# Attention block over 16 images: the next input is exchanged behind the outputs, its statistics move into the scores, and one reciprocal moves ahead of the outputs

## What is computed

```python
h    = group_norm(x, 32 groups) * gn_w + gn_b
q, k, v = split(qkv_w @ h + qkv_b)            # each 512 x 1024
attn = softmax((q.T @ k) / sqrt(512), axis=-1)
o    = out_w @ (v @ attn.T) + out_b
out  = x + o
```

## Time and profile before

| | |
|---|---|
| median of 3 runs | 1997.63 us (1994.39 to 1999.02) |
| profiled execution | 1995.93 us |
| its span, first to last instruction | 1994.1 us |
| TensorE matmul busy | 1977.3 us (99%) |
| TensorE weight load busy | 1679.2 us (84%) |
| VectorE, ScalarE, GpSimd busy | 1644.5 us (82%), 1121.0 us (56%), 448.8 us (23%) |
| granted TensorE clock | 1.000 |
| DMA, mean over the span | 79 GB/s |

### The profile page before, as it was taken

How to read it: one execution, slowest core, us unless ns; L and a number is a source line. 1 busy time by engine, 2 the same in 40 slices (tenths; PEclk the granted TensorE clock), 3 DMA queues, 4 the chain that set the end, 5 groups by cost and what they waited for, 6 DMA issues and landing times. The chain is left out here.

```text
span 1994.1 us, 26069 instructions
## 1 busy us (share of the span) xinstructions
PE 1977.3 (99%) x9895; PEld 1679.2 (84%) x9895; DVE 1644.5 (82%) x2010; ACT 1121.0 (56%) x1431; POOL 448.8 (23%) x306
## 2 busy tenths in 40 slices
PE   9999999999999999999999999999999999999999
PEld 7888888888888888888888888887888888878788
DVE  8896987969879698796978879697796987969866
ACT  6564645646465564645656467464565646556461
POOL 1122040231412213131230401314022131221311
PEclk9999999999999999999999999999999999999999
DMA  6305143060431504324042330614306043150411
GB/s 176 128 7 138 49 75 118 6 159 28 75 118 22 170 2 75 118 54 139 6 86 101 70 123 6 146 41 75 118 11 165 17 75 118 20 172 2 75 33 54
DMA packets 102637, 157.89 MB, mean 79 GB/s; under 512 B 49377, under 2 KB 51265, under 8 KB 102513
## 3 DMA queue, kind: packets, MB, share of 16 engines
q0 software_dynamic: 31264, 73.15, 17.5%
q1 hardware_dynamic: 71248, 83.08, 12.9%
HBM read 85.57 MB, written 68.26 MB: 77 GB/s over the span
## 5 line engine op out<-in xcount | busy, mean ns | idle before, releaser
L459 PE MATMUL ring<-r_hi 128*128 128x512 f32 (+1 forms) x1724 | 657.3, 381 | 0.6 <-ACT ring L932 0.4
L460 PE MATMUL ring<-r_lo,r_hi 128*128 128x512 f32 (+1 forms) x1724 | 656.4, 381 | 0.0
L461 PE MATMUL ring<-r_hi,r_lo 128*128 128x512 f32 (+1 forms) x1724 | 656.3, 381 | 0.0
L459 PEld LDWEIGHTS ring<-r_hi 128*128 128x128 f32 x1724 | 324.2, 188 | 64.1 <-DVE r_lo L1478 2.1
L461 PEld LDWEIGHTS ring<-r_hi,r_lo 128*128 128x128 f32 x1724 | 324.2, 188 | 62.0
L460 PEld LDWEIGHTS ring<-r_lo,r_hi 128*128 128x128 f32 x1724 | 324.3, 188 | 61.1
L881 ACT ACTIVATE stage<-ring,keybias 128x512 f32<-128x512 f32 x256 | 175.2, 685 | 164.2 <-PE ring L461 161.5
L1171 POOL PARTITION_ALL_REDUCE stage<-stage x32 | 127.2, 3976 | 460.3 <-DVE stage L1531 460.3
L854 ACT ACTIVATE stage<-ring,by_tile 128x512 f32<-128x512 f32 x120 | 82.5, 687 | 245.9 <-PE ring L461 245.9
L1463 DVE TENSOR_TENSOR r_lo<-stage,r_hi 128x1024 fp32r<-128x1024 f32 x128 | 182.1, 1452 | 0.0
L459 PE MATMUL ring<-h_hi,r_hi 128*128 128x512 f32 x444 | 172.8, 389 | 0.1
(11 more groups left out here) (199 smaller groups left out, 3903.0 us busy)
## 6 DMA issues: line engine op xcount, KB each, us to landing
xs<-x_in SPq DMA_DIRECT2D x64, 512.0 KB, 6.2
out<-xs SPq DMA_DIRECT2D x60, 512.0 KB, 5.4
out<-run_max POOLq DMA_DIRECT2D x60, 256.0 KB, 5.7
inv<-inv_row SPq DMA_DIRECT2D x32, 256.0 KB, 4.1
out<-spare POOLq DMA_DIRECT2D x30, 256.0 KB, 6.9
out<-all_max POOLq DMA_DIRECT2D x30, 256.0 KB, 5.1
r_hi<-g_dram POOLq DMA_DIRECT2D x15, 512.0 KB, 6.4
r_lo<-g_dram POOLq DMA_DIRECT2D x15, 512.0 KB, 6.5
```

Source lines behind the costliest of these rows:

```text
L459: nc.tensor.matmul(ps_out, st_hi, m_hi, start=first, stop=False, skip_group_check=goes_on)
L460: nc.tensor.matmul(ps_out, st_hi, m_lo, start=False, stop=False, skip_group_check=goes_on)
L461: return nc.tensor.matmul(ps_out, st_lo, m_hi, start=False, stop=last, skip_group_check=goes_on)
```

## The change

- `change_input` (store `xs`, wait, load the next image) is a function now. Image 0's exchange stays in its scores; that of every later image `b + 1` (up to image 14) comes behind `spread_inverses(b, 1)` and ahead of `key_bias(b + 1)` in SyncE's list, that is at the start of T.
- `shift_input` of image `b + 1` comes behind ScalarE's four `h_combined_part`, ahead of its T work.
- From image 1 on, the eight `stats_part` go between VectorE's first maxima in S; `group_variance` comes behind them; `group_std_part` goes between ScalarE's copies of S2 and S3; `group_root` and `group_spread` ahead of four maxima, `affine_pair` ahead of the subtractions.
- `inverse(b, 1)` comes ahead of the scaled outputs of half 0.
- GpSimd's `load_u` waits for the end of product S2 of the scores with all its four loads; two of them went after A12 before.

```diff
@@ -413,20 +413,24 @@
                 for at, name in ((0, "a11"), (1, "a12")):
                     sp.dma_start(by_rows(u_dram[side, :, at, :]), u_raw(t, name).bitcast(FP32)).then_inc(s_u_out, DMA)
 
+            def change_input(b):
+
+                for k in range(CT):
+                    sp.wait_ge(s_shifted, b * CT + k + 1)
+                    sp.dma_start(out_v[b, :, k, :], xs[:, k, :]).then_inc(s_sent[k], DMA)
+                for k in range(CT):
+                    sp.wait_ge(s_sent[k], (b + 1) * DMA)
+                    sp.dma_start(xs[:, k, :], x_v[b + 1, :, k, :]).then_inc(s_x[k], DMA)
+
             def store_u_s2():
                 for n, (side, t) in enumerate(((0, r_hi), (1, r_lo))):
                     sp.wait_ge((s_uhi, s_ulo)[n], 2)
                     sp.dma_start(u_dram[side, :, 2, :], t[:, u_home(1, S2), :].bitcast(FP32)).then_inc(s_us2_out, DMA)
 
             for b in range(B):
-                for k in range(CT):
-                    if b + 1 < B:
-                        sp.wait_ge(s_shifted, b * CT + k + 1)
-                        sp.dma_start(out_v[b, :, k, :], xs[:, k, :]).then_inc(s_sent[k], DMA)
+                if b == 0:
+                    change_input(0)
                 if b + 1 < B:
-                    for k in range(CT):
-                        sp.wait_ge(s_sent[k], (b + 1) * DMA)
-                        sp.dma_start(xs[:, k, :], x_v[b + 1, :, k, :]).then_inc(s_x[k], DMA)
                     group_stats(b + 1)
                 if b == 1:
                     store_u_s2()
@@ -434,6 +438,8 @@
                 spread_inverses(b, 0)
                 own_sums(b, 1)
                 spread_inverses(b, 1)
+                if b + 2 < B:
+                    change_input(b + 1)
                 if b + 1 < B:
                     key_bias(b + 1)
 
@@ -1009,11 +1015,14 @@
                     if k == 0:
                         act.wait_ge(s_bias_out, (b + 1) * DMA)
                     copy_scores(b, P_A12, k, k, k, s_c11, CT)
-                    shift_input(b, k)
+                    if b == 0:
+                        shift_input(b, k)
 
                 act.wait_ge(s_tlo, splits(b + 1))
                 for i in range(CT):
                     copy_scores(b, P_S2, i, i, 8 + i, s_p2)
+                if 0 < b < B - 1:
+                    group_std_part(b + 1)
                 if b == 0:
                     for n, (a, count) in enumerate(((S1, 5), (S2, 6), (S3, 7), (S4, 8))):
                         g_sum_part(a, n, count)
@@ -1024,9 +1033,8 @@
                     copy_scores(b, P_S3, i, CT + i, 12 + i, s_p3)
                 for i in range(CT):
                     copy_scores(b, P_A22, i, CT + i, CT + i, s_c21)
-                if b + 1 < B:
+                if b == 0:
                     group_std_part(b + 1)
-                if b == 0:
                     exponential(b, 0, 0)
                     p_part(b, 0, 0)
                     exponential(b, 0, 1)
@@ -1091,6 +1099,8 @@
 
                             act.wait_ge(s_unit, unit(b, "A") + CT)
                         h_combined_part(b + 1, c)
+                    for k in range(CT):
+                        shift_input(b + 1, k)
 
         @block.gpsimd
         def _(pool):
@@ -1139,7 +1149,7 @@
                     nc.gpsimd.dma_start(t[:, at:at + 2, :], g_dram[side, :, :, :]).then_inc(s_gload, DMA)
 
             def load_u(b):
-                pool.wait_ge(s_unit, unit(b, "S") + 4 * P_A12 + 4)
+                pool.wait_ge(s_unit, unit(b, "S") + 4 * P_S2 + 4)
                 count = 1 if b == 1 else 2
                 if b == 1:
                     pool.wait_ge(s_u_out, 4 * DMA)
@@ -1148,7 +1158,6 @@
                 at = u_home(b, A12)
                 for side, t in ((0, r_hi), (1, r_lo)):
                     nc.gpsimd.dma_start(t[:, at:at + count, :], u_dram[side, :, 1:1 + count, :]).then_inc(s_uload, DMA)
-                pool.wait_ge(s_unit, unit(b, "S") + 4 * P_S2 + 4)
                 for side, t in ((0, r_hi), (1, r_lo)):
                     nc.gpsimd.dma_start(t[:, u_home(b, A11), :], u_dram[side, :, 0, :]).then_inc(s_uload, DMA)
 
@@ -1660,14 +1669,22 @@
                     key_bias(b)
                     t_sum_rest(b, S2)
                     for i in range(1, CT):
+                        if more:
+                            stats_part(b + 1, 2 * i - 2)
+                            stats_part(b + 1, 2 * i - 1)
                         max_step(b, 0, i, i, s_c11, b * 4 + i + 1)
                     t_sum_rest(b, S3)
+                    if more:
+                        stats_part(b + 1, 6)
+                        stats_part(b + 1, 7)
                     t_sum_rest(b, S4)
                 if b == 1:
                     u_sums()
-                if more:
+                if b == 0:
                     for q in range(CT * NB):
                         stats_part(b + 1, q)
+                elif more:
+                    group_variance(b + 1)
                 if b == 0:
                     for n, a in enumerate((S1, S2, S3, S4)):
                         g_sum_rest(a, n)
@@ -1678,28 +1695,31 @@
                     add_scores(b, P_S1, i, 12 + i, s_p3, s_c22)
                     if i > 0:
                         max_step(b, 1, i, CT + i, s_c22, b * 4 + i + 1)
+                if b > 0 and more:
+                    group_root(b + 1)
+                    group_spread(b + 1)
                 for i in range(CT):
                     max_step(b, 0, CT + i, CT + i, s_c21, b * 4 + i + 1)
-                if more:
+                if b == 0:
                     group_variance(b + 1)
                 for i in range(CT):
                     add_scores(b, P_S4, i, 8 + i, s_p2, s_c12)
                     max_step(b, 1, CT + i, i, s_c12, b * 4 + i + 1)
+                if b > 0 and more:
+                    affine_pair(b + 1)
 
                 for q in range(CT):
                     subtract_max(b, 0, q)
-                if more:
+                if b == 0:
                     group_root(b + 1)
                     group_spread(b + 1)
-                if b == 0:
                     for q in range(CT):
                         p_rest(b, 0, q)
                         first_v_rest(q)
                     first_v_rest(4)
                     subtract_max(b, 1, 0)
                     subtract_max(b, 1, 1)
-                    if more:
-                        affine_pair(b + 1)
+                    affine_pair(b + 1)
                     first_v_rest(5)
                     sum_tree(b, 0)
                     first_v_rest(6)
@@ -1739,11 +1757,11 @@
                     for k in range(CT):
                         h_rest(b + 1, k)
                     h_combined(b + 1)
+                inverse(b, 1)
                 for c in range(CT):
                     scale_output(b, 0, c)
                     if not more:
                         whole_output(0, c)
-                inverse(b, 1)
                 if more:
                     for k in range(CT):
                         key_dot(b + 1, k)
```

## The result

The changed kernel took 2004.06 us (median of 10 runs, 2000.04 to 2005.6) against 1997.97 us for the kernel before on the same chip (10 runs, 1993.66 to 2003.14): ratio 1.0028, interval 1.0016 to 1.0040. It is slower, where a gain of 9 us was forecast. The profiled execution took 2000.42 us with a span of 1998.6 us, 4.5 us more than before.

A forecast was written before the change was run, and what follows sets the result against it. TensorE was taken as the bound, with only its waits to win. Gains of 8.3 + 2.0 + 0.5 us less 1.4 and 0.4 us gave 9.0 us: 1988.6 us, own range 1985 to 1993, whole range 1984 to 2010 us.

The forecast's parts named there:

- the 0.9 us net delay of the fourth add: In T, half 0's fourth add lands 0.9 us later because it shares the DMA engines with stores of x.
- stores meet the last two adds: In T, shifts end near 1250, so stores of x overlap only half 0's last two adds; fourth lands 1.2 to 1.4 us late.
- the term of 1.4 us: At T's third product, 0.1 us of added TensorE wait in each of 14 images, a cost of 1.4 us.
- The reciprocal, 8.3 us: Between images, inv comes up to 2.4 us earlier, removing 9 TensorE waits at T's second product and their restarts: 8.3 us.
- What is late next: At T's third product, the lo part behind the last scaled output, held by the all_max add, has 0.8 us of slack.
- The statistics, 2.0 + 0.5 us: Statistics in S no longer wait for x: 2.0 us of waits in V and 0.5 us at T's third product gained.
- The floor of 12 us: Only TensorE's waits, 10.7 us, and some 1.5 us of restarts can be won: about 12 us, 0.6%.
- Rival 2: In T, adds wait behind stores, delayed 2 us or more, so the third product waits: 2004 to 2018 us, chance 0.2.
- The row on `U`: Loads of U beside stores of x landed in 7.3 us, G's without x in 6.5: 0.8 us for 512 KB.
- The rule quoted for it: An add's 2 KB row stands behind more than one 4 KB row of x, so the delay is over 1.4 us.
- Rival 4: Half 1's sum, not the reciprocal's place, sets its time, so the 7.4 us of waits stay: 1995 us, chance 0.03.

The follow-up runs named there:

- e2: The changed kernel with the input exchange of T behind the key bias in SyncE's list instead of ahead; 1979.95 us, ratio 0.9908 to the kernel before.
- e10: The kernel before with only the input exchange moved to T, ahead of the key bias; 1989.9 us, ratio 0.9966.
- e12: The changed kernel with only the reciprocal of half 1 back behind half 0's scaled outputs; 1985.52 us, ratio 0.9953 to the kernel before.
- e9: The kernel before with only the input exchange moved to T, behind the key bias; 1982.39 us, ratio 0.9923.
- e6: The changed kernel with the exchange behind the key bias and the reciprocal back behind half 0's scaled outputs; 1979.52 us, ratio 0.9902 to the kernel before.
- e1: The kernel before with only the reciprocal of half 1 moved ahead of half 0's scaled outputs; 1997.67 us, ratio 1.0000.
- e8: The changed kernel with each store of x in T replaced by a load of the same 512 KB; 2004.12 us, one run, beside 1998.84 us before.
- e3: The changed kernel with the second combined tile's lo part ahead of half 1's third and fourth scaled outputs; 1988.9 us, ratio 0.9953 to the kernel before.

## Why the prediction was wrong

**The step that failed is the 0.9 us net delay of the fourth add**, priced from its own 1.6 us of engine time shared with the stores ("it lands 1.2 to 1.4 us late"), under the sentence "stores meet the last two adds". The shifts do end where the prediction put them, 5.3 us after the first scaled output. But the first store leaves at 2.9 us, when three adds are in flight, and the delays add up along the adds' queue: against e2, the second add lands 1.1 us later (10.1 against 9.0 us), the third 2.1 us (12.6 against 10.5 us), the fourth 3.4 us (15.3 against 11.9 us). From issue to landing the fourth took 8.8 us instead of the 5.5 us of before. So the term of 1.4 us was 17.3 us in listed waits.

A delay near the forecast's 1.4 us is what e10 and e12 show (1.5 us against e9, 1.8 us against e6), where the stores leave 7.5 us after the first scaled output and the fourth add alone is slowed. They stand behind the load of `inv` on SyncE's list, and the same change moves the reciprocal that this load waits for; the prediction did not look at that wait. It priced the two parts of the change one by one, and the loss lies in their combination: neither e1 (1.0000) nor e10 (0.9966) nor e12 (0.9953) is slower than before. How the 16 engines share their time between an add and `x` stays open.

**The reciprocal, 8.3 us**, was wrong in kind. It does remove the 9 waits for a scaled output, and e1 puts as many behind the `lo` part; e6 against e2 shows nothing. "What is late next" named the right place, the add of `all_max`, and gave 0.8 us of slack. It left out that VectorE's `lo` parts would be pushed into GpSimd's all-reduce, which costs 1.9 us in most images; the trace of before could have shown it, as both rows stand there.

**The statistics, 2.0 + 0.5 us**, had the right mechanism at a fraction of its size. VectorE sat 83.8 us in all for `x` before; with `x` there early, its first scaled output starts 10.4 us ahead of T instead of 9.0 us (e9), with the spread statistics 10.8 us (e2). That 1.4 us brings `inv` into T early enough in nearly every image. The prediction had VectorE 0.5 us earlier at the end of A; in the changed kernel it is 1.8 us (10.75 less 8.99). The early `x` was costed as the end of the waits in V and 0.5 us at the third product, when it was also what the 9 waits at the second product needed. e9 is worth 15 us by its ratio.

**The floor of 12 us** was read from idle time between records that overlap. Each restart hides 0.16 us where the prediction put 0.1 us, and starts that are late by less leave no idle time at all. 19.1 us were lost, and the versions with a late exchange in the table get 15.9 to 16.6 us of it back.

**Rival 2 was the one that happened**: the adds wait behind the stores, 2004 to 2018 us, measured 2004.06 us. It had the place and the waits right, and a chance of 0.2, since the row on `U` was taken as the nearer one. That its price fits is partly luck: by its rule, the delay less 0.8 us in 14 images, a delay of 3.4 us gives 2.6 times 14, 36 us, and a time near 2023 us. The `lo` part came only 1.9 us later than in e2 (6.7 against 4.8 us), since it now starts some 5 us into the all-reduce and takes its usual 1.22 us, where in e2 it starts 2.5 us into it and takes 3.1 us. The row on `U` has plain transfers beside plain transfers; an add beside `x` was nowhere in the trace. The rule quoted for it, that an engine alternates between its queues and drains whole packets (the Trainium skill, DMA: Bandwidth & Descriptors, Queues, rings and completion order), pointed the right way: the delay was over 1.4 us, and by e8 it is the same for loads and stores. That the engines took turns so, no run here shows.

Right were: the copies of S3 behind the table loads cost TensorE nothing from image 2 on (one wait of 1.2 us in image 1), the blocks of `G` and the key bias stayed hidden (the changed kernel lists no wait for either, with the blocks landing in 10.8 and 10.2 us), and V's waits went (5.2 us lost there before, 0.4 after). Rival 4 was not what happened: the row of reciprocals leaves 0.11 us after the first scaled output (1130.05 less 1129.94), before it was 2.59 us (1247.86 less 1245.27).

The best version is e2 or its equals: 1979.5 to 1980 us, 0.9% below the kernel before, and e6 reaches it without touching the reciprocal.

## What to carry to other kernels

When a transfer is moved, count all that is in flight when it leaves, since delays add up along a queue, and ask what stands ahead of it on its own queue and whether another part of the same change sets that free earlier. Where two waits end at nearly the same time, price the earlier of them at nothing until the second is shown to have slack, and run each part alone and the whole less each part. On an engine whose records overlap, count the loss from the distance of starts, not from the idle time listed.

## What was not expected of the hardware

After TensorE's longest wait, 3.67 us in image 2 of the changed kernel, the granted clock of the next 2 us was 0.50, that is 1.2 GHz. TensorE's matmuls there, and two stretches by windows (busy us and count of PE, PEld, DVE, ACT, POOL, then the granted clock, the DMA share and GB/s):

```profile
290.50 0.79 PE L465 MATMUL ring<-r_hi,g_hi 128*128 128x512 f32 x1 [3.67 <-DVE r_lo L1299]
291.10 0.63 PE L466 MATMUL ring<-r_lo,g_hi 128*128 128x512 f32 x1
291.52 0.63 PE L467 MATMUL ring<-r_hi,g_lo 128*128 128x512 f32 x1
...
293.54 0.39 PE L466 MATMUL ring<-r_lo,g_hi 128*128 128x512 f32 x1
```

```profile
291.00:293.00 2.00, 2.00 (x6) 1.52 (x6) 1.72 (x2) 0.00 (x0) 0.20 (x1) 0.50 1.06 406
294.00:297.00 3.00, 3.00 (x15) 2.46 (x14) 0.66 (x1) 0.84 (x2) 0.40 (x2) 1.00 1.08 282
```

The starts from 291.10 to 293.23 come about 0.43 us apart instead of 0.227 us, and image 2's T loses 5.3 us with a wait of 3.67 us. The other waits of the changed kernel have no such stretch behind them. In e1 and e3, whose longest waits are 2.1 and 2.4 us, image 2 has one too, and in e8 image 2 has one behind 3.9 us, but a wait of 2.7 us later in e8 has none (granted clock 1.00 behind it). So the length of the wait doesn't decide it alone; what does is open.

A `lo` part of VectorE took up to 5.67 us instead of 1.22 us when it started together with GpSimd's all-reduce (e3), while a scaled output, which reads PSUM, took its usual 0.69 us beside it (e1).
